# Loop control, two order changes and the last residual tiles in an fp32 linear-attention and feed-forward kernel

## The reference, cut to what matters

```
h = layernorm(x) * (1 + ca) + sa
x = x + ga * (linear_attention(h) @ W_out + b_out)      # 16 heads of 32, causal, running sums
h = layernorm(x) * (1 + cb) + sb
x = x + gb * ((silu(h @ wg.T) * (h @ wu.T)) @ wd.T)     # hidden width 1536
```

## Time and profile before

| | |
|---|---|
| median of 3 runs | 2127.78 us (2126.88 to 2130.28) |
| profiled execution | 2129.17 us, span of its instructions 2127.5 us |
| attention, groups 2 to 13 (TensorE's loop) | 793.05 us of it |
| feed-forward, one group in the loop | 126.7 us |
| mean granted TensorE clock | 0.995 |

### The profile page before, as it was taken

How to read it: one execution, slowest core, us unless ns; L and a number is a source line. 1 busy time by engine, 2 the same in 40 slices (tenths; PEclk the granted TensorE clock), 3 DMA queues, 4 the chain that set the end, 5 groups by cost and what they waited for, 6 DMA issues and landing times.

```text
span 2127.5 us, 41629 instructions
## 1 busy us (share of the span) xinstructions
PE 2061.2 (97%) x14832; PEld 1668.9 (78%) x14832; DVE 1581.8 (74%) x2151; ACT 1004.6 (47%) x1733; POOL 994.2 (47%) x791
## 2 busy tenths in 40 slices
PE   5999999999999999999979999999999999999998
PEld 4788887878878788788867878787887878878786
DVE  7998988988989889898785675757657575674743
ACT  5544454444544445445433643536445353643532
POOL 2644545545454454454554344443444444344444
PEclk9999999999999999999999999999999999999999
DMA  6111122221222212222156565554655546465452
GB/s 252 35 53 68 56 79 97 80 91 55 85 91 80 91 57 86 89 81 75 38 185 223 171 199 178 180 196 139 216 177 197 177 155 206 151 217 177 158 179 85
DMA packets 157164, 276.83 MB, mean 130 GB/s; under 512 B 11105, under 2 KB 35681, under 8 KB 157026
## 3 DMA queue, kind: packets, MB, share of 16 engines
q1 hardware_dynamic: 156498, 273.73, 39.0%
q10 hardware_dynamic: 528, 1.05, 0.1%
HBM read 208.67 MB, written 66.06 MB: 129 GB/s over the span
## 4 chain that ended last, share of the span: by engine, by line
PE 82%; DVE 9%; issue 4%; DMA 2%; ACT 1%; POOL 1%; SPq 0%; DVEq 0%; POOLq 0%; ACTq 0%
PE sc L1747 16%; PE pj L1073 15%; PE pj L1747 11%; PE sc L1147 8%; PE pj L1069 7%; PE sc L1804 6%; PE num L1125 3%; PE num L1804 3%; PE state L1804 3%; PE num L1118 3%; PE sc L1101 3%; DVE r_den L820 1%; PE sc L1111 1%; DVE xt_hi L1579 1%; PE sc L1033 1%
## 5 line engine op out<-in xcount | busy, mean ns | idle before, releaser
L1410 POOL TENSOR_TENSOR h_lo<-y_rows,h_hi 128x512 fp32r<-128x512 f32 x192 | 246.4, 1301 | 411.9 <-ACT h_hi L1502 411.9
L424 POOL TENSOR_TENSOR x_res<-y,x_res 128x512 f32<-128x512 f32 x64 | 81.9, 1280 | 310.6 <-DVE y L843 310.5
L820 DVE RECIPROCAL r_den<-r_den 128x512 f32<-128x512 f32 x64 | 213.8, 3340 | 0.0
L582 ACT ACTIVATE z_exp<-pj,qk_neg 128x512 f32<-128x512 f32 x128 | 88.1, 688 | 211.8 <-PE pj L1073 184.1
L825 DVE TENSOR_TENSOR probs<-sc,causal 128x512 f32<-128x512 f32 x256 | 158.3, 679 | 1.3 <-PE sc L1101 1.1
L1073 PE MATMUL pj<-xt_hi,w_hi 128*128 128x512 f32 x512 | 151.0, 416 | 5.3 <-ACT xt_hi L574 3.5
L1804 PE MATMUL sc<-wd,h_hi 128*128 128x512 f32 x384 | 151.9, 396 | 0.0
L1804 PE MATMUL sc<-wd,h_lo 128*128 128x512 f32 x384 | 149.7, 390 | 0.0
L1614 DVE TENSOR_TENSOR r_den<-pj,k_tok 128x512 f32<-128x512 f32 x96 | 66.2, 690 | 106.8 <-ACT k_tok L1485 54.6
L1480 ACT ACTIVATE k_tok<-sc 128x512 f32<-128x512 f32 x96 | 56.2, 585 | 179.0 <-PE sc L1747 179.0
L1073 PE MATMUL pj<-xt_lo,w_hi 128*128 128x512 f32 x512 | 138.9, 393 | 0.9 <-DVE xt_lo L792 0.9
(11 more groups left out here) (246 smaller groups left out, 5654.3 us busy)
## 6 DMA issues: line engine op xcount, KB each, us to landing
w_hi<-parts SPq DMA_DIRECT2D x48, 1024.0 KB, 5.2
w_lo<-parts SPq DMA_DIRECT2D x48, 1024.0 KB, 5.2
x_mid<-x_res SPq DMA_DIRECT2D x96, 256.0 KB, 2.1
x_res<-in_L_attn_x SPq DMA_DIRECT2D x64, 256.0 KB, 3.5
x_res<-x_mid SPq DMA_DIRECT2D x64, 256.0 KB, 3.9
full<-x_mid SPq DMA_DIRECT2D x64, 256.0 KB, 3.1
xg<-in_L_attn_x SPq DMA_DIRECT2D x15, 1024.0 KB, 7.6
parts<-r_den SPq DMA_DIRECT2D x48, 256.0 KB, 2.3
```

Of the source, the lines that this page charges most:

```text
L820: dve.reciprocal(r_den[parity][:, c, :], r_den[parity][:, c, :]).then_inc(rden_ready, 1)
L1410: pool.tensor_tensor(out=h_lo[b], in0=h[i], in1=h_hi[b].bitcast(F32), op=ALU.subtract).then_inc(h_lo_ready, 1)
```

## The change

It has four parts.

1. TensorE's hardware loop over attention groups 2 to 13 becomes a Python loop, so that the twelve groups are written out in its stream, with constants for addresses and semaphore values.
2. In feed-forward groups 0 to 6, `gate_y(G, 8)` stands before the second and third sum (T2, T3) of the next group's second half and no longer behind them.
3. In the same groups, `add_c11(G + 1, 0)` stands before `gate_y(G, 14)` and no longer behind it.
4. In the last group the residual tiles 8 to 15 are loaded into the eight x buffers. GpSimd adds tiles 8 to 14 there (`late_residual`), VectorE adds tile 15 itself behind its gating, and SyncE stores from there (`load_late`, `store_late`). A new semaphore, `last_ready`, tells SyncE of tile 15.

```diff
-        with pe.Fori(1, NG // 2 - 1) as pair:
-            group(pair * 2, 0)
-            front(pair * 2 + 1, 1, 0)
-            group(pair * 2 + 1, 1)
-            front(pair * 2 + 2, 0, 0)
+        for g in range(2, NG - 2):
+            group(g, g % 2)
+            front(g + 1, (g + 1) % 2, 0)
...
+        def load_late(t):
+
+            wait(sp, y_out[t % 4], (FG - 1) * 64 + 16 * (t // 4 + 1))
+            sp.dma_start(xg[t], tile_of(mid_tiles, (FG - 1) * FT + t)).then_inc(xr_in[t % 4], 16)
+
+        def store_late(t):
+            if t < FT - 1:
+                wait(sp, y_ready, (FG - 1) * 16 + FT + t + 1)
+            else:
+                sp.wait_ge(last_ready, 1)
+            sp.dma_start(tile_of(out_tiles, (FG - 1) * FT + t), xg[t]).then_inc(y_out[t % 4], 16)
...
+                if last and half:
+                    for t in range(4):
+                        load_late(t)
+                    for t in range(FT):
+                        store_late(t)
+                        if t < 4:
+                            load_late(t + 4)
+                    continue
                 for t in range(FT):
                     i = half * FT + t
                     store(G, i)
-                    if not last or i + 3 < 16:
+                    if not last or i + 3 < FT:
                         load_residual(G, i + 3)
...
+        def late_residual(t):
+            pool.wait_ge(y_gated, (FG - 1) * 16 + FT + t + 1)
+            pool.wait_ge(xr_in[t % 4], (FG - 1) * 64 + 32 + 16 * (t // 4 + 1))
+            pool.tensor_tensor(out=xg[t], in0=y[t % 2], in1=xg[t], op=ALU.add).then_inc(y_ready, 1)
...
-            for i in range(FT, 2 * FT):
-                residual(G, i)
+            if ahead:
+                for i in range(FT, 2 * FT):
+                    residual(G, i)
+            else:
+                for t in range(FT - 1):
+                    late_residual(t)
...
                 for i in range(FT, 2 * FT):
                     gate_y(G, i)
+                dve.wait_ge(y_gated, FG * 16)
+                dve.wait_ge(xr_in[3], FG * 64)
+                dve.tensor_tensor(out=xg[FT - 1], in0=y[1], in1=xg[FT - 1], op=ALU.add).then_inc(last_ready, 1)
                 return
...
             sum_of(G + 1, T1, 1)
+            gate_y(G, FT)
             sum_of(G + 1, T2, 1)
             sum_of(G + 1, T3, 1)
-            gate_y(G, FT)
             sum_of(G + 1, T4, 1)
...
-            for i in range(FT + 4, FT + 7):
+            for i in range(FT + 4, FT + 6):
                 gate_y(G, i)
             add_c11(G + 1, 0)
-            gate_y(G, FT + 7)
+            for i in range(FT + 6, FT + 8):
+                gate_y(G, i)
```

More of the change, by code:

```diff
@@ L1290, in feed_forward @@
         sem("g1_ready"), sem("g2_ready"), sem("h1_ready"), sem("h2_ready"), sem("h_hi_ready"), sem("h_lo_ready"))
+    last_ready = sem("flast_ready")
     dn_ps, y_gated, y_ready, dve_passed = sem("dn_ps"), sem("fy_gated"), sem("fy_ready"), sem("fdve_passed")
```

## The result

| | before | after |
|---|---|---|
| median of 6 runs each, us | 2126.9 (2122.37 to 2130.28) | 2109.25 (2108.88 to 2110.86) |
| profiled execution: time, span, us | 2129.17, 2127.5 | 2109.39, 2107.6 |

The ratio is 0.9922 (the two medians alone would give 0.9917), interval 0.9912 to 0.9933: faster by 17.7 us on medians, where 24.2 were forecast off the profiled execution. The direction and the larger part of the size are right. 0.9922 of the 2127.78 us shown is 2111.2 us, above the range's upper end of 2109.5.

The account below looks back on a forecast made before the run. TensorE, busy 97% of the span, was taken as the bound. Terms 16.2 + 0.8 + 2.9 + 4.3 = 24.2 us gave 2105.0 off the profiled execution, 2103.6 off the median; forecast 2104.3 us, range 2098.5 to 2109.5.

Parts of the forecast that it names:

- Part 1, the attention loop: TensorE's twelve looped attention groups: written out, neither jump stalls nor the slow clock behind them remain, 16.2 us less.
- the lower bound for it, 9.9: Attention loop: 9.9 us gained if only the gaps go and something else takes the rest.
- The rival of a new wait in the attention: Attention: other engines' jumps or VectorE at 89% show, the 6.3 us behind the gaps aren't gained, 2110.6 us; chance 0.09.
- Part 2, the gating of tile 8: Feed-forward `down`: the 0.9 us wait moves from tile 12 to tile 13; seven groups gain 0.8 us.
- The first rival: Feed-forward `down`: tile 13 doesn't wait, so the gating's move gains 6.3 us instead of 0.8, 2098.8 us; chance 0.14.
- The rival of one more blocked instruction per group: VectorE, feed-forward: T2 or T3 blocked as well as a low part, 7.7 us worse, 2112 us; chance 0.06.
- Part 3, the first sum: Feed-forward group changes: with the sum ahead of tile 14's gating, TensorE's wait before `p6` goes, 2.9 us less.
- the upper bound: First sum: 3.8 us gained if the restart behind a wait costs another 0.12 us each.
- Part 4, the tail: End of kernel: loads come early, VectorE adds tile 15 behind its gating, store takes 2.5 us; 4.3 us less.
- The lower bound of 3 for "crowded stores": Tail: only 3 us gained if tile 15's load or crowded stores take another 1.3 us.
- Its own range: The forecast's own range, 2101 to 2107 us: bounds of parts 3 and 4, and 1.6 us for a slow-clock stretch.
- Straight code: Written-out attention groups: rival that instruction fetch stalls TensorE, slower, up to 156 us more, 2260 us; chance 0.02.

Follow-up runs that it names:

- b1: The changed kernel with the gating of tile 8 put back behind the two sums; 2108.73 us, ratio 0.9913.
- b2: The changed kernel with the gatings of tiles 9, 10 and 11 moved ahead too; 2103.67 us, ratio 0.9891.
- c1: The changed kernel with the rows of feed-forward group G + 2 loaded early, in the second half of group G; 2103.90 us, ratio 0.9888.
- d1: The changed kernel with rows loaded early as in c1, but parts 2 and 3 taken back; 2109.33 us, ratio 0.9916.
- a3: The kernel before with only the last eight residual tiles in the x buffers and the last add on VectorE; 2122.43 us, ratio 0.9984.
- a4: The kernel before with its attention loop as three passes of four groups, two jumps back instead of five; 2120.07 us, ratio 0.9972.
- b4: The changed kernel with TensorE's feed-forward loop written out as well; 2110.29 us, ratio 0.9925.

## Why the prediction was right or wrong

**Part 1, the attention loop: mechanism right, size wrong for the median.** In the profile the term is exact: 777.02 us against 776.9, no "issue" wait, no clock under 1 there. The step that failed is "12 x 64.74 = 776.9, so the loop loses 16.2 us", taken as if every execution lost that. What the loop loses is 16.2, 13.2 or 9.0 us in three executions, since the gaps vary and a slow clock behind them comes three times, once or never. On medians it is 11.5. The prediction had the lower bound for it, 9.9, and the row that warned: the gaps sum to only 9.9, and most of the other 6.3 hung on the clock (the groups behind three of the jumps take 66.3 to 66.5 us without a gap in them, 5.1 us together; the rest is mainly what a gap is shown too short, 5 x 0.16). It corrected the start of its sum by 1.4 us for the execution shown, half of it, but not the term. The rival of a new wait in the attention, whose time is near to what came, is wrong as a mechanism: there is none. Its 2110.6 being near is luck.

**Part 2, the gating of tile 8: right at each step.** The wait went from tile 12 to tile 13, at 5.7 us in place of 5.3; T3 became the blocked instruction. At its own place it gives the forecast 0.8 us (65.3 to 64.5); in the whole stretches of b1 and after it can't be told. The first rival, its full 6.3 us, fell here; b2 shows that those microseconds are there, for whoever moves all the gatings (9.0 us at the place, 5.7 with the rows late). The rival of one more blocked instruction per group is wrong too: at each of the seven changes VectorE has five instructions of some 1.8 us in place of 0.68, before and after (b2 has four).

**Part 3, the first sum: the wait went and gave 3.8 us, the upper bound, but the rows took most of it back.** The 2.9 was too small, since the matmul behind the restarted one comes 0.1 us late too, which the bound of 3.8 had allowed for. The step that failed is "it isn't later, and nobody waits for it but the store". The gating wasn't the only thing behind the sum. VectorE runs on into the statistics of the next group's rows, and those are loaded behind the last stores of this group. VectorE came earlier to a transfer that didn't, its wait rose from 9.7 to 12.7 us, the rest of the stretch grew by 3.1, and parts 2 and 3 together gave 1.5 us instead of 3.7. With rows early they give 4.5 (c1 and d1). The wait of 9.7 us stood in the profile of before, on an engine that was not the bottleneck, and the prediction has no term for it.

**Part 4, the tail: mechanism right, size wrong twice.** VectorE's add stands right behind its gating as forecast. The step that failed is "store 2.5, end 2123.2": that is what the last store took in before, and in after it took 3.6, with the new order of loads and stores. 1.1 us is the whole shortfall of this term in the profile. The lower bound of 3 for "crowded stores" had named it. And the piece that is removed was read from one execution: it took 8.66 us there, but 7.8 in the mean of the four profiles with the old tail. a3, the part alone, gave 2.0 us on medians.

**The 1.8 us at the start** lie in a part that is the same in both programs; they are chance between executions (148.2 to 151.2 us in thirteen profiles of the same code), and belong to the profiled execution alone. The prediction's range allowed one stretch of slow clock, 1.6 us, but at the change to feed-forward. Its own range ended at 2107, while the terms it names come to 2104.3 + 1.1 + 1.3 + 1.6 = 2108.3 if all fall the slow way.

**Straight code didn't starve TensorE.** In the same 669 us as the earlier trace rows, the instruction queue has this many packets in after:

```profile
q8 instruction: 54, 0.88, 0.6%
```

All are hidden: no "issue" wait is left. That rival was rightly given little.

## What to carry to other kernels

Before a loss is priced from one execution, compare the same loop in several: where it stands on gaps that vary or on the clock, the median's gain (11.5 us here) is nearer the mean over executions (12.8 in three) than what the one shown lost (16.2). When an engine is made earlier, look for its next wait even if it is not the bottleneck: a wait for a load whose issue stands behind other work takes the gain, and it must be moved with it. And waits in a chain hide each other: remove them together (12.7 us) before you judge one by what it gives alone (5.7 and 3.4).

## What was not expected of the hardware

- The same jump back of the same loop costs TensorE from 1.3 to 2.6 us of gap, and the drop to 1.2 GHz behind it for some 3.4 us comes in some executions and not in others: three, one and none of five jumps. The three came with gaps of 2.0 to 2.6 us, but the longest gap of a3, 2.6 us, brought none. In code that both kernels share, a drop of 3.4 us came at 71 us in before and at 82 us in after.
- Kernels without that jump vary by 0.8 to 4.9 us in four to six runs each, with it by 10 in 25 (before). With two jumps one varies by 11 in ten runs (a4), and that stays open.
- A loop of TensorE that jumps back without loss gains nothing from being written out: 946.80 us in b4 against 944.07 in after, with 22 more packets of instructions and no "issue" wait.
- The last store takes 2.4 to 2.5 us from the end of the add to the end of the span in four kernels with one order of loads and stores, and 2.9 to 3.6 in eight with another.
